# Packing queries and keys into every fourth partition, with fewer transfers and one row of maxima

## What is computed

```python
q = (x @ wq).reshape(B, S, NH, HD)      # NH = HD = 16
k = (ctx @ wk).reshape(B, Skv, NH, HD)  # ctx = x in self-attention
v = (ctx @ wv).reshape(B, Skv, NH, HD)
scores = jnp.einsum("bqhd,bkhd->bhqk", q, k) * HD ** (-0.5)
attn = jax.nn.softmax(scores, axis=-1)
out = jnp.einsum("bhqk,bkhd->bqhd", attn, v).reshape(B, S, NH * HD) @ wo
```

## Time and profile before

| | |
|---|---|
| median of 3 runs | 1216.24 us |
| lowest and highest | 1204.12 and 1219.71 us |
| profiled execution, its own time | 1218.36 us |
| its span, first to last instruction | 1216.3 us |
| mean granted TensorE clock | 0.909 of full speed |
| TensorE busy | 1038.8 us (85%) |
| VectorE, ScalarE, GpSimd busy | 652.6, 613.9, 246.5 us |

### The profile page before, as it was taken

How to read it: one execution, slowest core, us unless ns; L and a number is a source line. 1 busy time by engine, 2 the same in 40 slices (tenths; PEclk the granted TensorE clock), 3 DMA queues, 4 the chain that set the end, 5 groups by cost and what they waited for, 6 DMA issues and landing times.

```text
span 1216.3 us, 22981 instructions
## 1 busy us (share of the span) xinstructions
PE 1038.8 (85%) x8556; PEld 844.9 (69%) x8556; DVE 652.6 (54%) x1523; ACT 613.9 (50%) x1300; POOL 246.5 (20%) x303
## 2 busy tenths in 40 slices
PE   3365788889999999999999999999999999988874
PEld 2244467677877777777777777877777777777762
DVE  3233253454747475756566574747474756545432
ACT  3141434356464646565655656564646465553432
POOL 2000001111213122222131312213131222132331
PEclk9566677889999999999999999999999999998986
DMA  4513243434242433434343535342423434303000
GB/s 159 86 35 47 47 53 56 56 47 62 42 63 33 72 38 68 53 55 64 55 64 46 73 46 73 47 66 41 61 35 69 46 51 61 48 13 47 12 9 9
DMA packets 76599, 64.10 MB, mean 53 GB/s; under 512 B 20288, under 2 KB 76005, under 8 KB 76520
## 3 DMA queue, kind: packets, MB, share of 16 engines
q1 hardware_dynamic: 76520, 63.04, 34.6%
HBM read 16.18 MB, written 4.19 MB: 17 GB/s over the span
## 4 chain that ended last, share of the span: by engine, by line
PE 52%; SPq 17%; DMA 14%; DVE 8%; ACT 4%; issue 3%; POOL 0%; DVEq 0%; ACTq 0%; POOLq 0%
PE ring L893 13%; PE mring L893 10%; DMA kpk_sa<-kT 9%; SPq L442 8%; SPq L452 8%; PE ring L950 6%; PE od L984 6%; DMA kpk_ca<-kT 4%; PE down_ps L1034 4%; DVE mx_sa L738 3%; PE mring L1107 2%; PE ring L970 2%; ACT qT L578 2%; PE mring L1083 2%; PE ring L901 1%
## 5 line engine op out<-in xcount | busy, mean ns | idle before, releaser
L605 ACT ACTIVATE probs<-ring 128x1024 f32<-128x1024 f32 (+1 forms) x192 | 190.9, 1021 | 45.8 <-PE ring L970 43.9
L738 DVE TENSOR_REDUCE mx_sa<-ring 128x4 f32<-128x1024 f32 x128 | 152.9, 1220 | 58.6 <-PE ring L950 58.2
L485 POOL TENSOR_TENSOR hidT_lo<-hid,hidT_hi 128x256 fp32r<-128x256 f32 x128 | 93.3, 735 | 295.7 <-ACT hidT_hi L634 295.7
L950 PE MATMUL ring<-kpk_sa,qpk_sa 48*128 48x256 f32 x512 | 69.4, 354 | 68.0 <-DMA kpk_sa<-kT 47.2
L743 DVE TENSOR_REDUCE mx_ca<-ring 128x4 f32<-128x308 f32 x128 | 55.4, 475 | 108.8 <-PE ring L950 108.8
L950 PEld LDWEIGHTS ring<-kpk_sa,qpk_sa 48*128 48x128 f32 x512 | 42.1, 204 | 93.5 <-DMA kpk_sa<-kT 50.6
L984 PE MATMUL od<-probs,vz_sa 128*32 128x256 f32 x1024 | 82.1, 446 | 0.2
L1034 PE MATMUL down_ps<-down_hi,hidT_hi 128*128 128x256 f32 x256 | 81.6, 319 | 0.0
L626 ACT ACTIVATE hid<-mring 128x256 f32<-128x256 f32 x128 | 47.6, 382 | 62.1 <-PE mring L893 61.9
L1034 PE MATMUL down_ps<-down_lo,hidT_hi 128*128 128x256 f32 x256 | 74.1, 289 | 0.0
L1034 PE MATMUL down_ps<-down_hi,hidT_lo 128*128 128x256 f32 x256 | 74.0, 289 | 0.0
(11 more groups left out here) (226 smaller groups left out, 2615.8 us busy)
## 6 DMA issues: line engine op xcount, KB each, us to landing
qpk_sa<-qT SPq DMA_DIRECT2D x96, 128.0 KB, 4.4
kpk_sa<-kT SPq DMA_DIRECT2D x96, 128.0 KB, 7.0
qpk_ca<-qT SPq DMA_DIRECT2D x96, 128.0 KB, 4.7
x_sb<-x SPq DMA_DIRECT2D x16, 256.0 KB, 2.7
x_res<-x SPq DMA_DIRECT2D x16, 256.0 KB, 2.7
out<-o_sb SPq DMA_DIRECT2D x16, 256.0 KB, 2.2
kpk_ca<-kT SPq DMA_DIRECT2D x96, 39.0 KB, 4.1
ctx_sb<-ctx SPq DMA_DIRECT2D x16, 77.0 KB
```

The lines of the kernel that those rows point to most:

```text
L485: nc.gpsimd.tensor_tensor(hidT[1][:, m % HID, :], hid[:, m % 2, :], hidT[0][:, m % HID, :].bitcast(F32), ALU.subtract).then_inc(S["hidlo"] ...
L605: nc.scalar.activation(granule(g, tag)[0:rows_, i0:i0 + 2, :, :].rearrange("p i h t -> p h i t"), ring_tile(("E", tag, k))[0:rows_].rearra ...
L738: nc.vector.tensor_reduce(mx[tag][:, :, :, k].rearrange("p q h -> p h q"), ps[:].rearrange("p h (q t) -> p h q t", t=T), AX_X, ALU.max).th ...
L950: last = mm(ps[:, half, col:col + kw], qpk[tag][r, slot, q * P:(q + 1) * P], kpk[tag][r, slot, :], start=True, stop=True)
```

## The change

- In self-attention queries and keys share one tile `qkT` and one packed tile `qk_sa`. A transfer takes queries and keys of one chunk, 128 partitions by two parts by 256 tokens (256 KB), and writes partitions j, j + 4, j + 8, ..., 32 of them over both halves, with four slots in each. There are three for each chunk (j = 0, 1, 2), so six for twelve. They are issued by `pack_qk`, in two steps `pqk.sa.0` and `pqk.sa.1`, each with its own semaphore. Both wait for the low parts of queries and keys. Scores 0 to 3 wait for the first, 4 to 7 for the second.
- In cross-attention three transfers of queries (256 KB) and three of keys (78 KB) take the place of six and six (128 KB and 39 KB), also into every fourth partition. Keys go ahead of queries.
- Partitions 3, 7, ... of each half hold zeros in the queries and ones in the keys, cleared once at the start, so GpSimd has two clears more. The last of them in each half (63 and 127) takes the negated maximum. `scores` multiplies 63 rows, `shifted` 64.
- The maxima are no longer split: one rounded row in place of two, one VectorE instruction and one transfer less for each attention.
- The columns of wq and wk are put in another order on the host, and the slots of cross-attention are numbered otherwise (`SLOT_AT`).
- All five lists of `ORDER` are rewritten. Those of SP and PE are shown.

```diff
 ORDER = {
     "sp": """
-        mr.sa@1 ldr@1 pq.ca@0 wl.8@2 wl.4@4 wl.0@5 pk.ca@0 ldcl@-1 ldx@3 mr.ca@0 wl.7@3 ldc@1 wl.9@2 st@-3 wl.1@5 pq.sa@2 wl.2@5 wl.5@4 wl.3@5 pk.sa@2 wl.6@4
-        wl.10@2
+        wl.10@1 mr.sa@1 wl.7@2 wl.0@5 ldcl@-1 wl.4@3 wl.1@5 pk.ca@0 pq.ca@0 wl.8@2 mr.ca@0 ldx@3 wl.5@3 st@-3 wl.2@5 ldr@1 wl.9@2 pqk.sa.0@2 wl.3@5 ldc@2
+        wl.6@3 pqk.sa.1@2
     """,
 ...
     "pe": """
-        pv.ca.0@-1 s2@-3 cT.ca@0 aT.sa@0 pv.ca.1@-1 v.ca@0 wo.sa@0 oT.ca@-1 dnp.5@-2 S.sa.0@1 nXT@-2 aT.ca@-1 dnp.6@-2 dnp.7@-2 S.sa.1@1 wo.ca@-1 S.sa.2@1
-        p2T@-3 S.sa.3@1 S.sa.4@1 pv2@-3 S.sa.5@1 T.mlp@-1 v.sa@1 S.sa.6@1 S.sa.7@1 gu.0@-1 T.ca@0 gu.1@-1 maxT.sa@1 qk.ca@0 gu.2@-1 dnp.0@-1 E.sa.0@1 E.sa.1@1
-        gu.3@-1 nFT@-2 dnp.1@-1 E.sa.2@1 E.sa.3@1 pv.sa.0@1 sc@-2 E.sa.4@1 gu.4@-1 E.sa.5@1 S.ca.0@0 pv.sa.1@1 gu.5@-1 S.ca.1@0 E.sa.6@1 pv.sa.2@1 pT@-2
-        E.sa.7@1 S.ca.2@0 h4@-2 dnp.2@-1 S.ca.3@0 T.sa@2 pv.sa.3@1 f2@-2 maxT.ca@0 gu.6@-1 qk.sa@2 dnp.3@-1 E.ca.0@0 gu.7@-1 E.ca.1@0 oT.sa@1 nCT@-2 dnp.4@-1
-        E.ca.2@0 E.ca.3@0
+        gu.7@-2 E.ca.2@-1 nCT@-3 oT.sa@0 pv.ca.0@-1 E.ca.3@-1 s2@-3 cT.ca@0 aT.sa@0 pv.ca.1@-1 v.ca@0 oT.ca@-1 wo.sa@0 aT.ca@-1 dnp.5@-2 S.sa.0@1 dnp.6@-2
+        dnp.7@-2 S.sa.1@1 wo.ca@-1 S.sa.2@1 p2T@-3 nXT@-2 S.sa.3@1 S.sa.4@1 pv2@-3 S.sa.5@1 T.mlp@-1 S.sa.6@1 v.sa@1 gu.0@-1 S.sa.7@1 T.ca@0 gu.1@-1 maxT.sa@1
+        qk.ca@0 gu.2@-1 dnp.0@-1 E.sa.0@1 E.sa.1@1 gu.3@-1 nFT@-2 E.sa.2@1 E.sa.3@1 pv.sa.0@1 sc@-2 E.sa.4@1 gu.4@-1 pv.sa.1@1 E.sa.5@1 S.ca.0@0 gu.5@-1
+        S.ca.1@0 E.sa.6@1 pT@-2 dnp.1@-1 E.sa.7@1 S.ca.2@0 pv.sa.2@1 h4@-2 S.ca.3@0 gu.6@-1 T.sa@2 maxT.ca@0 f2@-2 pv.sa.3@1 qk.sa@2 dnp.2@-1 dnp.3@-1
+        E.ca.0@0 dnp.4@-1 E.ca.1@0
     """,
 }
 ...
-        qT = sb("qT", [P, C, 2, T], F32R)
-        kT_all = sb("kT", [P, C, 2, T], F32R)
+        qkT = sb("qkT", [P, C, 4, T], F32R)
         KW = {"sa": T, "ca": SKV2}
-        kT = {t: kT_all[:, :, :, 0:KW[t]] for t in KW}
+        qT = qkT[:, :, 0:2, :]
+        kT = {t: qkT[:, :, 2:4, 0:KW[t]] for t in KW}
         SLOTS = 2 * PAIRS
-        qpk = {t: sb(f"qpk_{t}", [P, SLOTS, T], F32R) for t in KW}
-        kpk = {t: sb(f"kpk_{t}", [P, SLOTS, KW[t]], F32R) for t in KW}
-        ROWS_S, ROWS_E = 3 * HD, 3 * HD + 2
+        qk_sa = sb("pk_sa", [P, SLOTS, 2, T], F32R)
+        qpk = {"sa": qk_sa[:, :, 0, :], "ca": sb("qpk_ca", [P, SLOTS, T], F32R)}
+        kpk = {"sa": qk_sa[:, :, 1, :], "ca": sb("kpk_ca", [P, SLOTS, SKV2], F32R)}
+        SLOT_AT = {"sa": lambda c, i: PAIRS * c + i, "ca": lambda c, i: C * i + c}
+        BAND = P // (2 * HD)
+        HALF = P // 2
+        MAX_ROW = HALF - 1
 ...
-        nm = {t: sb(f"nm_{t}", [P, QT, 2, 2, SLOTS]) for t in KW}
-        mT = sb("mT", [4 * SLOTS, T], F32R)
+        nm = {t: sb(f"nm_{t}", [P, QT, 2, SLOTS]) for t in KW}
+        mT = sb("mT", [2 * SLOTS, T], F32R)
 ...
+        PACKS = {"sa": (3, 3), "ca": (6, 0)}
 ...
-                           ("pqk", 192), ("S", fills), ("mx", 8), ("nm", 2),
-                           ("maxT", 1), ("mT", 1), ("mr", 32), ("E", fills), ("exp", fills), ("pv", 4 if t == "sa" else 2), ("o", 2),
+                           ("pk0", 16 * PACKS[t][0]), ("pk1", 16 * PACKS[t][1]), ("S", fills), ("mx", 8), ("nm", 1),
+                           ("maxT", 1), ("mT", 1), ("mr", 16), ("E", fills), ("exp", fills), ("pv", 4 if t == "sa" else 2), ("o", 2),
 ...
-                "qkT": lambda: [(S[tag, "pqk"], 192)],
-                "mT": lambda: [(S[tag, "mr"], 32)],
+                "qkT": lambda: [(S[tag, "pk0"], 16 * PACKS[tag][0])] + ([(S[tag, "pk1"], 16 * PACKS[tag][1])] if tag == "sa" else []),
+                "mT": lambda: [(S[tag, "mr"], 16)],
@@ -433,32 +438,34 @@
                 sp.wait_ge(S["o"].sem, S["o"].at(n, 1))
                 sp.dma_start(o_v[n], o_sb[:]).then_inc(stored.sem, 16)
 
-            def pack_q(n, tag):
-
-                sp.wait_ge(S[tag, "qklo"].sem, S[tag, "qklo"].at(n, 1))
-                for half in range(2):
-                    for j, part in enumerate((0, 1, 0)):
-                        r = 64 * half + HD * j
-                        sp.dma_start(qpk[tag][r:r + HD].bitcast(F32), qT[:, half, part, :].bitcast(F32)).then_inc(S[tag, "pqk"].sem, 16)
-
-            def pack_k(n, tag):
+            def pack_qk(n, tag, c):
 
                 if at_first(n):
                     sp.wait_ge(s_cset, 6)
                 sp.wait_ge(S[tag, "qklo"].sem, S[tag, "qklo"].at(n, 2))
-                for half in range(2):
-                    for j, part in enumerate((0, 0, 1)):
-                        r = 64 * half + HD * j
-                        sp.dma_start(kpk[tag][r:r + HD].bitcast(F32), kT[tag][:, half, part, :].bitcast(F32)).then_inc(S[tag, "pqk"].sem, 16)
-
-            def max_rows(n, tag):
+                for j, parts in enumerate((slice(0, 3, 2), slice(0, 4, 3), slice(1, 3))):
+                    sp.dma_start(qk_sa[j:P:BAND, PAIRS * c:PAIRS * (c + 1)].bitcast(F32), qkT[:, c, parts, :].bitcast(F32)).then_inc(S[tag, f"pk{c}"].sem, 16)
+
+            def pack_q(n, tag):
+
+                if at_first(n):
+                    sp.wait_ge(s_cset, 8)
+                sp.wait_ge(S[tag, "qklo"].sem, S[tag, "qklo"].at(n, 1))
+                for j, part in enumerate((0, 0, 1)):
+                    sp.dma_start(qpk[tag][j:P:BAND].bitcast(F32), qT[:, :, part, :].bitcast(F32)).then_inc(S[tag, "pk0"].sem, 16)
+
+            def pack_k(n, tag):
+
+                sp.wait_ge(S[tag, "qklo"].sem, S[tag, "qklo"].at(n, 2))
+                for j, part in enumerate((0, 1, 0)):
+                    sp.dma_start(kpk[tag][j:P:BAND].bitcast(F32), kT[tag][:, :, part, :].bitcast(F32)).then_inc(S[tag, "pk0"].sem, 16)
+
+            def max_row(n, tag):
 
                 sp.wait_ge(S[tag, "mT"].sem, S[tag, "mT"].at(n, 1))
-                for half in range(2):
-                    r = 64 * half + ROWS_S
-                    sp.dma_start(qpk[tag][r:r + 2].bitcast(F32), mT[2 * SLOTS * half:2 * SLOTS * (half + 1), :].bitcast(F32)).then_inc(S[tag, "mr"].sem, 16)
-
-            run(sp, "sp", {"wl": load_w, "ldx": load_x, "ldr": load_res, "ldc": load_ctx, "ldcl": load_ctx_l, "st": store, "pq": pack_q, "pk": pack_k, "mr": max_rows})
+                sp.dma_start(qpk[tag][MAX_ROW:P:HALF].bitcast(F32), mT[:].bitcast(F32)).then_inc(S[tag, "mr"].sem, 16)
+
+            run(sp, "sp", {"wl": load_w, "ldx": load_x, "ldr": load_res, "ldc": load_ctx, "ldcl": load_ctx_l, "st": store, "pqk": pack_qk, "pq": pack_q, "pk": pack_k, "mr": max_row})
             sp.wait_ge(stored.sem, stored.at(B - 1, 16))
 
 
@@ -469,8 +476,10 @@
             pool.wait_ge(s_cset, 1)
             nc.gpsimd.affine_select(out=ident[:], in_=ident[:], compare_op=ALU.not_equal, fill=1.0, base=0,
                                     pattern=[[-1, P]], channel_multiplier=1).then_inc(s_cset, 1)
+            nc.gpsimd.memset(qpk["sa"][:].bitcast(F32), 0.0).then_inc(s_cset, 1)
             nc.gpsimd.memset(kpk["sa"][:].bitcast(F32), 1.0).then_inc(s_cset, 1)
             nc.gpsimd.memset(vz["sa"][:, :, :, HD:32], 1.0).then_inc(s_cset, 1)
+            nc.gpsimd.memset(qpk["ca"][:].bitcast(F32), 0.0).then_inc(s_cset, 1)
             nc.gpsimd.memset(kpk["ca"][:].bitcast(F32), 1.0).then_inc(s_cset, 1)
             nc.gpsimd.memset(vz["ca"][:, :, :, HD:32], 1.0).then_inc(s_cset, 1)
             for p in range(2):
@@ -592,7 +601,7 @@
 
                 act.wait_ge(S[tag, "maxT"].sem, S[tag, "maxT"].at(n, 1))
                 reuse(act, "mT", ("maxT", tag), n)
-                nc.scalar.activation(mT[:], ring_tile(("maxT", tag))[0:4 * SLOTS, 0, 0:T], ACT.Copy).then_inc(S[tag, "mT"].sem, 1)
+                nc.scalar.activation(mT[:], ring_tile(("maxT", tag))[0:2 * SLOTS, 0, 0:T], ACT.Copy).then_inc(S[tag, "mT"].sem, 1)
 
             def exps(n, tag, k):
                 act.wait_ge(S[tag, "E"].sem, S[tag, "E"].at(n, k + 1))
 ...
-                        nc.vector.tensor_reduce(mx[tag][:, :, half, 2 * k:2 * k + 2].rearrange("p q i -> p i q"),
+                        nc.vector.tensor_reduce(mx[tag][:, :, half, 2 * C * (k % 2) + k // 2:2 * C * (k % 2) + k // 2 + C + 1:C].rearrange("p q i -> p i q"),
                                                 v, AX_X, ALU.max).then_inc(S[tag, "mx"].sem, 1)
 
             def maxsplit(n, tag):
                 dve.wait_ge(S[tag, "mx"].sem, S[tag, "mx"].at(n, 8))
-                nc.vector.tensor_scalar(nm[tag][:, :, :, 0, :].bitcast(F32R), mx[tag][:], -1.0, None, ALU.mult).then_inc(S[tag, "nm"].sem, 1)
-                dve.wait_ge(S[tag, "nm"].sem, S[tag, "nm"].at(n, 1))
-                nc.vector.scalar_tensor_tensor(out=nm[tag][:, :, :, 1, :], in0=mx[tag][:], scalar=-1.0, in1=nm[tag][:, :, :, 0, :],
-                                               op0=ALU.mult, op1=ALU.subtract).then_inc(S[tag, "nm"].sem, 1)
+                nc.vector.tensor_scalar(nm[tag][:].bitcast(F32R), mx[tag][:], -1.0, None, ALU.mult).then_inc(S[tag, "nm"].sem, 1)
 
```

(16 more changed lines are left out.)

22 lines of the change are left out of this document (11 added, 11 removed).

## The result

The changed kernel takes 1126.55 us (median of 4 runs, 1122.68 to 1127.15) against 1217.97 us for the kernel before beside it: a ratio of 0.928 (95% interval 0.920 to 0.936). The profiled execution took 1126.34 us, its span 1124.4, with a mean granted clock of 0.947 for 0.909. The forecast was 1145 in a range of 1116 to 1188.

A forecast was written before the change was run, and what follows sets the result against it. PE was taken to bound the kernel, busy 1038.8 of 1216.3 us, with 75.6 us of waits for packed keys. Eight steps summed to -72.7 us, giving 1145 us, range 1116 to 1188.

The forecast's parts named there:

- Self-attention pack: Packing of self-attention queries and keys: half a pack takes 4.3 us, scores can begin 10 us sooner.
- step 1: First pack, at the start: issue to scores falls from 15.3 to 4.9 us, -10.4 us.
- The transfers are no faster: Rival on the pack transfers: half a pack takes 7.5 us, 1155 us in all; counted inside the forecast's 0.62.
- Steps 1 to 4, 6 and 8: First pack -10.4, second batch -8.3, packs 120 to 250 -11, fill max rows -2.5, new fill waits +4, tail -8 us.
- step 7: Steady part, 11.6 periods: pack waits -3.0, clock -0.8, new VectorE and ScalarE waits +1.0 a period; -32.5 us.
- step 5: Clock in the fill: 2.4 GHz reached sooner with less idle; -4 us, between 0 and some 12 to gain.
- step 8: Tail from 960: cross-attention key waits of 6.7 us and two max rows go, -8 us.
- The four orders: Rewritten lists: waits could be added; the half pack behind the context load, 4.7 us against 13.7, was taken as hidden.
- What would show it: Signs if right: pack waits under 5 us, landing within 3, first scores near 38, period 61 to 63, clock 0.7.
- The idle changes its name: Rival: PE meets VectorE and ScalarE instead of packs, 2 us a period come back, 1185 us; chance 0.28.
- The second half of the pack is late: Rival: half pack in SP's queue takes over 13.3 us and PE waits each period; some 1275 us, chance 0.05.
- Zero for 63 and 64 rows: PE's score matmuls: 63 and 64 rows in place of 48 and 50 cost nothing.

The follow-up runs named there:

- The experiments on partitions and number of transfers: Kernel before with six 256 KB self-attention transfers to 16 neighbouring partitions: 1250.91 us; kernel after with twelve of 128 KB to every fourth partition: 1125.22 us.
- the kernel with one packing: Kernel with the new packing and the old lists, but cross-attention packed as before by twelve transfers to neighbouring partitions: 1158.65 us, ratio 0.960.

## Why the prediction was right, and where it was off

*Part "Self-attention pack": 4.3 us for half a pack.* Right: issue to scores took 4.1 us. The first pack was issued 1.9 us later than before, though, where the prediction had 0.6, so step 1 gave 9.3 us for 10.4. With the old lists it was issued at 32.57, so the delay comes from the new lists, and the two clears on GpSimd cost nothing, as said. The experiments on partitions and number of transfers show the cause that the earlier trace rows only suggested. "The transfers are no faster" falls. They also bear out the rule of the Trainium skill ("SBUF — State Buffer", "Door 1: The DMA port swizzle"), which the sum did not lean on: with six transfers of the same 256 KB issued together, a median landing of 9.4 us became 2.7.

*Idle, all steps without the clock.* Steps 1 to 4, 6 and 8 and the 3.0 - 1.0 of step 7 make -10.4 - 8.3 - 11 - 2.5 + 4 - 8 - 23.2 = -59.4. Measured: 121.0 - 177.5 = -56.5. In the fill -31.4 was forecast for -31.1. That the whole fits so well is in part luck: ten periods gave -24.4 for a forecast of -20, the tail only -3.2 for -8, and the start +2.1, of which step 1 counts 0.6.

*Clock, step 5 and the 0.8 of step 7: the term that was mis-sized.* They make -4 - 9.3 = -13.3; measured were -35.4: 18.7 in the fill, outside even the bound of 12, 10.1 in ten periods for a forecast of 8, and 6.2 in the tail, where step 8 had none. These 22 us are the whole miss of the sum, which came to -72.7 for -91.9, with 3 us of idle the other way. The bound was the error, and it didn't follow from the earlier trace rows: if the clock of a window is taken as that of its busy time, 39.58 us at 0.59 hold some 16 us that a full clock would give back, and 56.83 at 0.84 another 9 (an estimate from these rows). Nor is 177.5 us "all that can go without touching the matmuls", as the first paragraph of the prediction has it: 35.4 went from the busy time of the same 8556. The likely reason is that the waits for packs, scattered over all batches, held the clock down; no run changes the clock alone. The runs do show how the two go together: taking away 28.5 us of idle from the kernel with one packing took 22.3 us of busy time with it; from the kernel before to that one it was 39.6 and 19.7. With half to four fifths of the idle added for the clock, in place of steps 5 and 7's 0.8, the sum would have come to 1112 to 1129; that is known only after the runs.

*Step 7, the steady part.* 3.45 us a period for 2.8. The +1.0 "for waits on VectorE and ScalarE that show once the packs don't stand in front" came, but from `xn_a`, and without the move of `bC` it would not have: waits of PE in window 500 to 960 of the kernel after are

```profile
PE ring L907 <- DVE xn_a L720: 6.7, 8, 0.9
PE ring L958 <- DVE mx_sa L747: 3.1, 8, 0.4
PE ring L899 <- DVE mx_sa L747: 2.0, 8, 0.3
PE ring L978 <- ACT probs L614: 1.4, 3, 0.5
```

Maxima and exponentials, named as what is late next, end 6.5 us of idle here, and 6.9 in the earlier trace rows.

*The four orders.* I priced them by SP's and PE's queues and found nothing. I didn't follow GpSimd's, where `bC` moved past `ms.ca`; that move cost 10 to 12 us, and the new lists 18 in all. It is luck that this brought the time into the range: the packing alone, at 1108, lies below the low end of 1116, in the main since the gain in clock was priced too low.

*What would show it.* The period (61 to 63), the landing (under 3 us), the first scores (38) and the place of the halves came as named. Two signs were missed narrowly: the wait for packs is 6.2 us, not under 5, since the first pack has nothing to hide behind, and the clock of the window 50 to 115 is 0.68, not 0.7.

*Rivals.* "The idle changes its name" is what `xn_a` does, at 0.9 us a period instead of 2, so in kind it came and in size it didn't. "The second half of the pack is late" didn't bind: each transfer of the half lands in some 3 us, against 13.3 for the half. Its price was also mis-added: 4.6 us in 15 periods on top of 1216 is 1285, not 1275. *Zero for 63 and 64 rows:* right, the group of the first pass took 349 ns for 354 and of the second 326 for 335.

## What to carry to other kernels

When idle goes from the engine that bounds the kernel, look at its granted clock before pricing the idle alone: each microsecond of scattered waiting for packs went with another half to four fifths of one in slower work here, and in the new order without the packing with four (62.5 for 14.6), so the sum of the idle alone doesn't give the price. For transfers from SBUF to SBUF, look at which partitions are written before the number and size of the transfers. And when an in-order list is rewritten, every engine's list is to be walked, for what now runs at the same time as well as for what now waits.

## What was new of the hardware

- A VectorE pass of 346 ns over 128 x 256 took up to 1431 ns while GpSimd ran passes of 1.3 us with operands in SBUF. The reduction from PSUM beside the first of them (at 580.05) kept its 1.21 us. The Trainium skill ("SBUF — State Buffer", "Who interferes with whom") has this as a lock on a port pair that both engines use, held for the whole instruction, which a VectorE `tensor_scalar` like this pass can run into and a `tensor_reduce` never does on this chip; the mean of 981 ns for 346 and the end of the passes 0.15 us behind GpSimd's fit it.
- Six transfers of 256 KB from SBUF to SBUF, issued 0.66 us apart, landed 2.5 to 3.0 us after their issue when they wrote every fourth partition, and 4.6 to 12.8 us when they wrote 16 neighbouring ones (window 500 to 900).
- The same 8556 matmuls were busy for 994.0 us in the least case among these kernels (mean clock 0.948) and 1101.3 in the most (0.861).
- Work added only to hold the clock up early didn't help later: 1.00 for 0.86 up to 50 us, but 0.79 for 0.85 in the window 115 to 180.
